# A transformer block on one core: four engines' orders laid anew, with scores between the two turned blocks of a unit

## The reference, cut to what matters

```python
def attn_ref(x, Wqkv, Wo):             # x: 32 x 256 x 128, 8 heads of 64
    qkv = einsum('bte,fe->btf', x, Wqkv)
    q, k, v = split(qkv.reshape(B, T, H, 3 * D), 3)   # then heads first
    q, k = q + pe, k + pe
    scores = einsum('bhtd,bhsd->bhts', q, k) / sqrt(D)
    probs = softmax(where(causal, scores, -inf))
    return einsum('btf,ef->bte', einsum('bhts,bhsd->bhtd', probs, v), Wo)

def ffn_ref(x, w, a1, a2, bias):
    return tanh(x @ w @ a1 @ a2 + bias)

x = x + layernorm(attn_ref(layernorm(x), Wqkv, Wo))
x = x + layernorm(ffn_ref(layernorm(x), w, a1, a2, bias))
```

## Time and profile before

| | us |
|---|---|
| median of 3 runs | 556.6 (556.47 to 557.93) |
| the profiled execution | 557.18 |
| its span, first to last instruction | 555.3 |
| TensorE busy | 523.5 (94%) |
| VectorE busy | 468.8 (84%) |
| ScalarE busy | 410.9 (74%) |
| GpSimd busy | 398.9 (72%) |

### The profile page before, as it was taken

One profiled execution on the slowest core, in us unless ns is written; L12 is line 12 of the kernel. 1 busy time (PEld: TensorE's weight loads), 2 busy tenths in 40 slices (PEclk: granted clock), 3 DMA queues, 4 the chain that ended last, 5 costly groups with the idle time before them and its releaser, 6 DMA issues.

```text
span 555.3 us, 18471 instructions
## 1 busy us (share of the span) xinstructions
PE 523.5 (94%) x5363; PEld 427.2 (77%) x5363; DVE 468.8 (84%) x2063; ACT 410.9 (74%) x1507; POOL 398.9 (72%) x650
## 2 busy tenths in 40 slices
PE   8799999999999999999999999999999999999771
PEld 4588888788888878888887887888788888878650
DVE  4988898888889888888988888898888889888723
ACT  2777878778787877878787787877778787777730
POOL 3535777777777777777778777777877777785644
PEclk9999999999999999999999999999999999999966
DMA  5100011100001010000101010010000001100000
GB/s 161 30 2 21 11 31 30 30 19 28 20 18 28 28 28 19 28 26 12 28 28 28 19 28 21 17 28 28 28 19 28 26 12 28 28 19 12 21 11 19
DMA packets 27964, 14.57 MB, mean 26 GB/s; under 512 B 1699, under 2 KB 27430, under 8 KB 27942
## 3 DMA queue, kind: packets, MB, share of 16 engines
q1 hardware_dynamic: 27510, 13.51, 8.5%
q10 hardware_dynamic: 432, 0.79, 0.4%
HBM read 10.09 MB, written 4.19 MB: 26 GB/s over the span
## 4 chain that ended last, share of the span: by engine, by line
PE 82%; ACT 9%; issue 4%; DVE 3%; DMA 1%; POOL 1%; ACTq 0%; POOLq 0%; DVEq 0%
PE turned_and_heads L935 17%; PE scores L881 15%; PE misc_bank L996 11%; PE turned_and_heads L921 9%; PE qk_bank L896 6%; ACT probs L265 5%; PE qk_bank L898 4%; PE qk_bank L897 4%; PE misc_bank L867 4%; PE misc_bank L979 3%; PE misc_bank L869 3%; PE misc_bank L868 3%; ACT vals L275 2%; ACT pt L285 1%; PE misc_bank L977 1%
## 5 line engine op out<-in xcount | busy, mean ns | idle before, releaser
L265 ACT ACTIVATE probs<-scores,neg_max 128x256 f32<-128x256 f32 (+1 forms) x512 | 209.3, 428 | 32.0 <-DVE neg_max L633 31.9
L633 DVE CUSTOM_DVE_ANT_0 scores<-scores,mask 128x256 f32<-128x256 f32 (+1 forms) x512 | 166.2, 386 | 3.2 <-PE scores L881 0.9
L643 DVE TENSOR_TENSOR qk<-qk_bank,pe 128x512 f32<-128x512 f32 x128 | 87.4, 683 | 32.9 <-PE qk_bank L898 25.3
L881 PE MATMUL scores<-qk 64*128 64x256 f32 (+1 forms) x1024 | 107.2, 337 | 5.5 <-ACT probs L265 2.5
L423 POOL TENSOR_TENSOR probs<-probs,inv_sum 128x512 f32<-128x512 f32 x126 | 101.6, 827 | 12.8 <-DVE inv_sum L649 12.8
L265 ACT ACTIVATION_READ_ACCUMULATOR probs<-scores,neg_max 128x1 f32 x512 | 108.8, 213 | 0.0
L881 PEld LDWEIGHTS scores<-qk 64*128 64x128 f32 x1024 | 88.5, 188 | 16.0 <-issue 9.8
L935 PE MATMUL turned_and_heads<-pt,vals 128*64 128x256 f32 (+1 forms) x1024 | 99.3, 337 | 1.5 <-ACT pt L285 1.5
L935 PEld LDWEIGHTS turned_and_heads<-pt,vals 128*64 128x64 f32 x1024 | 64.8, 138 | 28.3 <-issue 2.8
L283 ACT COPY pt<-turned_and_heads 128x512 f32<-128x512 f32 x128 | 76.7, 599 | 11.1 <-PE turned_and_heads L921 11.0
L896 PE MATMUL qk_bank<-xt_hi,w_hi 128*128 128x256 f32 x256 | 81.2, 317 | 2.0 <-DVE qk L643 1.2
(11 more groups left out here) (87 smaller groups left out, 863.2 us busy)
## 6 DMA issues: line engine op xcount, KB each, us to landing
x_in<-in_x SPq DMA_DIRECT2D x32, 128.0 KB, 2.2
x_res<-in_x SPq DMA_DIRECT2D x32, 128.0 KB, 2.1
out_x<-x SPq DMA_DIRECT2D x32, 128.0 KB, 1.8
w_raw<-in_w_qkv_t ACTq DMA_DIRECT2D x3, 256.0 KB, 3.7
pe<-pe_table SPq DMA_DIRECT2D x1, 256.0 KB, 5.6
wo<-in_w_o_t SPq DMA_DIRECT2D x1, 256.0 KB, 4.0
mask<-causal_mask SPq DMA_DIRECT2D x1, 128.0 KB, 5.5
w_sb<-in_w SPq DMA_DIRECT2D x2, 64.0 KB, 3.8
```

The lines of the kernel that those rows point to most:

```text
L265: ins = nc.scalar.activation(probs[k][j][:, h, lo:hi], s_bank[j][:, h, lo:hi], ACT.Exp, bias=neg_max[k][j][:, i:i + 1], scale=-1.0, accum_ ...
L633: ins = nc.vector.tensor_tensor_reduce(some, some, mask[:, t * P:2 * P], -1.0, HIGHEST, ALU.add, ALU.min, neg_max[k][j][:, i:i + 1])
L643: nc.vector.tensor_tensor(qk[j][:, :], qk_bank[:, :], pe[:, :], ALU.add).then_inc(qk_kept, 1)
L881: ins = mm(s_bank[j][:, h, at:at + k_hi], qk[j][r, q_lo:q_lo + P], qk[j][r, T:T + k_hi], start=(at == 0), stop=True, skip_group_check=True)
```

## The change

In the period, TensorE's order becomes, for k = 0: qk(1,0), heads of unit 0 of the batch before, values, qk(1,1), turned block, scores, turned block, transposes of x and y, heads of unit 1, feed-forward, qk of the next batch; and for k = 1: projection, qk, turned block, scores of the next batch, turned block, values. Scores now stand between the two turned blocks of a unit. ScalarE takes over the scaling of pair 0 (`scale_probs`, four instructions a unit), VectorE all copies of heads. The orders of ScalarE, VectorE and GpSimd are rearranged to suit; VectorE's `drain()` goes. The start loads the weights' first two parts through SyncE and four other things through ScalarE's queue behind one small exponential, and takes the low part of the first x before the second weight remainder. The end is written anew, with more warm-up matmuls, the last projection into `qk_bank` in place of `misc_bank`, and without its wait for batch 30's tanh.

```diff
@@ scalar @@
+            act.wait_ge(zeros_set, 2)
+            nc.scalar.activation(touched[:, :], eps[:, :], ACT.Exp)
+            act.dma_start(ident[:, :], ident_dram).then_inc(ident_in, 16)
...
+            def scale_probs(b, k):
+                act.wait_ge(inv_found, pairs(b, k, 1))
+                for t, (lo, hi) in enumerate(((0, T), (T, SC))):
+                    for h in range(2):
+                        some, i = probs[k][0][:, h, lo:hi], 2 * t + h
+                        ins = nc.scalar.mul(some, some, inv_sum[k][0][:, i:i + 1])
+                ins.then_inc(scaled[0], 1)
...
             def slot(b, k):
                 if k == 0:
+                    scale_probs(b.plus(-1), 0)
+                    exps(b.plus(-1), 1, 1)
+                    keep_attn(b.plus(-2))
+                    keep_turned(b.plus(-1), 0, 0)
+                    scale_probs(b.plus(-1), 1)
                     keep_turned(b.plus(-1), 0, 1)
...
@@ vector @@
-            def scale_probs(b, k):
-                dve.wait_ge(inv_found, pairs(b, k, 1))
...
-            def keep_heads(b):
+            def keep_heads(b, k):
...
             def slot(b, k):
                 if k == 0:
+                    stats_x(b.plus(2))
+                    stats_attn(b.plus(-2))
...
@@ tensor @@
             def slot(b, k):
                 if k == 0:
                     make_qk(b, 1, 0)
+                    make_heads(b.plus(-1), 0)
                     make_vals(b, 1)
+                    make_qk(b, 1, 1)
                     turn_probs(b.plus(-1), 1, 0)
-                    make_qk(b, 1, 1)
-                else:
+                    make_scores(b, 1)
+                    turn_probs(b.plus(-1), 1, 1)
                     turn_x(b.plus(1))
                     turn_y(b.plus(-2))
...
@@ tensor, end @@
                 make_attn(last.plus(-1), 1)
+                warm_up(4, qk_bank, 256)
                 make_heads(last, 0)
+                warm_up(4, qk_bank, 256)
                 turn_probs(last, 1, 0)
```

More of the change, by code:

```diff
@@ L217, in _ @@
             load(first, x_in, x_loaded)
-            sp.dma_start(ident[:, :], ident_dram).then_inc(ident_in, 16)
+            for i in range(2):
+                part = slice(i * F, (i + 1) * F)
+                sp.dma_start(w_raw[:, part], w_qkv_t[:, part]).then_inc(w_in[i], 16)
             sp.dma_start(pe[:, :], pe_dram).then_inc(pe_in, 16)
-            sp.dma_start(mask[:, :], mask_dram).then_inc(mask_in, 16)
             load(first.plus(1), x_in, x_loaded)
@@ L286, in keep_turned @@
                                turned_banks[:, :, T:T + P].rearrange("p f (n c) -> p n f c", c=D)).then_inc(pt1_kept, 1)
-            def keep_heads(b):
-                if not b.exists():
-                    return
-                act.wait_ge(heads_made, units(b, 2))
-                wait(act, attn_made, b.times(1, -1))
-                nc.scalar.copy(heads_t[b.parity][:, 2:4, :], heads_bank[:, :].rearrange("p (j t) -> p j t", j=2)
-                               ).then_inc(heads_kept[1], 1)
             def keep_x_hi(b):
@@ L378, in end @@
                 keep_y(last.plus(-1))
-                keep_heads(last)
                 tanh(last.plus(-1))
@@ L486, in slot @@
                 if k == 0:
-                    rstd_attn(b.plus(-2))
                     make_x1(b.plus(-2))
@@ L490, in slot @@
                     norm_y(b.plus(-2))
-                    norm_ffn(b.plus(-3))
+                    make_out(b.plus(-3))
                 else:
+                    norm_x(b.plus(2))
                     scale_probs(b, 0)
-                    make_out(b.plus(-3))
-                    norm_x(b.plus(2))
+                    norm_ffn(b.plus(-2))
+                    rstd_attn(b.plus(-1))
             def split_bias():
@@ L524, in end @@
             def end():
-                rstd_attn(last.plus(-2))
+                make_out(last.plus(-3))
                 make_x1(last.plus(-2))
@@ L529, in end @@
                 norm_y(last.plus(-2))
-                norm_ffn(last.plus(-3))
-                make_out(last.plus(-3))
                 scale_probs(last, 0)
@@ L534, in end @@
                 make_x1(last.plus(-1))
+                norm_ffn(last.plus(-2))
                 norm_y(last.plus(-1))
-                norm_ffn(last.plus(-2))
                 make_out(last.plus(-2))
@@ L725, in scale_last @@
             def scale_last():
+                dve.wait_ge(scaled[1], units(last, 1))
                 dve.wait_ge(inv_found, pairs(last, 1, 2))
@@ L742, in stats_attn_last @@
                 dve.wait_ge(attn_made, B)
-                take_stats("attn", last, misc_bank[:, 0:T].rearrange("p (t e) -> p t e", t=TT))
+                take_stats("attn", last, qk_bank[:, 0:T].rearrange("p (t e) -> p t e", t=TT))
             def norm_attn_last():
@@ L788, in begin @@
                 take_w_rest(0)
+                keep_x_lo(first)
                 take_w_rest(1)
-                keep_x_lo(first)
-                stats_x(first.plus(1))
                 take_w_rest(2)
@@ L794, in begin @@
                 keep_qk(first, 0, 0)
+                stats_x(first.plus(1))
                 wait_stats("x", first.plus(1))
@@ L838, in end @@
                 moments_last("y", last)
+                stats_ffn(last.plus(-1))
                 moments_last("ffn", last.plus(-1))
@@ L892, in make_qk @@
                 for part in range(2):
+                    if b.is_first() and k == 0 and j == 0:
+                        pe_eng.wait_ge(w_hi_made, part + 1)
+                        pe_eng.wait_ge(w_lo_made, part + 1)
                     p = 2 * k + j
@@ L981, in make_ffn, with make_attn_last @@
                 ins.then_inc(ffn_made, 1)
+            def make_attn_last():
+                pe_eng.wait_ge(heads_kept[0], B)
+                pe_eng.wait_ge(heads_kept[1], B)
+                pe_eng.wait_ge(qk_kept, 4 * B)
+                for t in range(TT):
+                    for p in range(PAIRS):
+                        ins = mm(qk_bank[:, t * E:(t + 1) * E], heads_t[1][:, p, t * P:(t + 1) * P], wo[:, p, :],
+                                 start=(p == 0), stop=(p == PAIRS - 1))
+                ins.then_inc(attn_made, 1)
             def make_attn(b, t):
```

187 lines of the change are left out of this document (89 added, 98 removed).

## The result

| | before | changed |
|---|---|---|
| median of 6 runs each | 557.43 (556.47 to 560.17) | 553.19 (552.12 to 553.95) |
| the profiled execution | 557.18 | 553.95 |
| its span | 555.3 | 552.1 |
| start: to the first projection | 36.51 | 42.07 |
| period, mean of 29 | 16.20 | 16.06 |

The ratio is 0.9918, with a 95% interval of 0.9892 to 0.9943. The kernel is faster by 0.8%. I had forecast 2.2%: the direction is right and the size is not (553.19 still lies inside the stated range of 535 to 554, at its upper edge). The three lower rows say where the difference lies (negative is faster): start +5.6 where the sum had 0, periods 29 x -0.14 = -4.1 where it had -6.7, end -4.6 where it had -5.2. Together -3.1; the spans differ by -3.2, the same to rounding.

The account below looks back on a forecast made before the run. TensorE's ring of some 18 blocks was taken as the bound. Span 555.3, periods -6.7, start 0, end -5.2 gave 543.4; plus 1.9 outside the span, less 0.6 to the median, 544.7; forecast 544.5 us, range 535 to 554.

Parts of the forecast that it names:

- Net 0, bounds -1.5 and +1.5: Start: first qk block some 0.8 us earlier from loading, first turned block about 0.9 later, cancelling out.
- (a): Values of t=0 on TensorE no longer wait for ScalarE's attn copy: -0.19 us a batch.
- (b): Scores of unit 1 no longer wait for unit 0's second exponentials: -0.36 us a batch.
- (c): TensorE neighbours: fewer array-shape changes at seams between scores, turned, projection and qk blocks; together -0.31 us a batch, bounds 0 and -0.45.
- (d): New TensorE stall before heads of unit 1, behind turned block and ScalarE's pt copies (chain 1.59): +0.51 us, bounds 0.4 and 0.7.
- (e): Unit 1's first turned block waits for VectorE's heads_t copy: +0.14 us a batch, bounds 0 and 0.4.
- (f): ScalarE scaling pair 0: 0.36 and 0.26 per instruction, 2.5 us a batch, hidden by scores and values, costing nothing.
- My three terms, -2.2, -3.5 and -0.4: End: shorter stretch before last heads -2.2; full-clock blocks to last projection -3.5; closing chain's two short TensorE blocks 0.4.
- Small waits everywhere with a clock that falls in the end: Rival: small waits at five places, clock falling in the end; period 16.1, end -2, about 551.5 us; chance 0.20.
- The slower rival: GpSimd's root steps delay VectorE's chain up to the heads_t copy; at 0.6 late period 16.6, 563 us; chance 0.10.
- Rival 3: Neighbouring TensorE blocks' shapes don't count, seam savings fall away; period 16.34, 555.5 us, no change; chance 0.07.
- rivals 1 and 2: No new stall: period 15.6, about 534.5 us, chance 0.14; small waits everywhere: about 551.5, chance 0.20.

Follow-up runs that it names:

- e5_half_pt: Changed kernel with ScalarE's first copy of turned weights for unit 1's second pair halved (stale numbers there); span 542.1 us, period 15.86.
- e4_heads_copy: Changed kernel with VectorE's copy of unit 0's heads moved before the y statistics and one reciprocal moved; 548.10 us, ratio to before 0.9813.
- e8_half_scale: Changed kernel with ScalarE scaling only the 128-column parts of pair 0, the other parts' factor left out; 552.30 us, period 16.07.
- e6_cold_end: Changed kernel without the end's six groups of warm-up matmuls; 553.28 us, end 45.4 against 44.3.
- e9_warm_end: Changed kernel plus first-slot warm-ups, first-slot VectorE reorder, earlier heads copy and more end warm-ups; 542.94 us, against 544.18 without the extra end warm-ups.
- e2_dve_start: Changed kernel with VectorE's first slot alone reordered: first row_max earlier, second qk copy between the two row_max; 549.30 us.

## Why the prediction was wrong in size

**The step that failed is the start.** The prediction put it as "Net 0, bounds -1.5 and +1.5". It measured +5.6 in the one profile and, from first scores on, +5.5 and +3.7 in the two. I had named the cause of the second gap (x_lo behind two row_max) and that scores of unit 1 stand ahead, and priced them at 0.9. The first and longer gap, of 2.54, I had not seen: on VectorE the qk copy stands behind the statistics and the maxima of both pairs. The order's part was 1.6, and the earlier loads gave nothing back: the first qk block started 0.5 earlier, but its second half waited for the weight remainder and the first scores began 0.1 later than before. What I had not priced at all is what an idle TensorE in a start costs beyond the gap itself: the clock, another 2.1 to 3.9. I had looked at the clock only for the end, where it had fallen before. With the start at the mean of these two measurements, +4.6, the forecast would have been 549.1; with the misses of the period (2.6) and of the end (0.6) it would have been 552.3, 0.9 from the median.

**The period, -0.14 where I had -0.23.** Point by point, by the table above:

- (a) held: values follow their turned block 0.52 later and no longer 0.72, -0.20 (forecast -0.19).
- (b) and scores in (c) held: -0.56 (forecast -0.54). Scores take 1.38 start to start.
- The rest of (c) was too good. The turned blocks' opening gap is not half a seam each: they gained 0.05 in all beyond (a), not 0.10. The projection gained 0.17, not 0.09, but the qk block behind it gives 0.07 back (0.88 where its like takes 0.81), and the two values blocks cost 0.03 more. Each seam is real; how it divides between the two blocks was guessed.
- (d) held: turned block to heads 1.60 (forecast 1.59), and e5_half_pt shows that it is this chain.
- (e) had the right place and was too small: 0.19 where I had 0.14. e4_heads_copy shows it.
- (f) held: 0 for the period, by e8_half_scale. Its size was low: four records run 1.48, and the next instruction starts 1.38 behind the first (218.34 to 219.72), where I had 1.24. The Trainium skill (ScalarE: Activation LUTs, section What ACT_TABLE_LOAD costs), which the prediction names beside its 0.36 without using it, would have given it: 280 ns + 0.833 ns a column with one pointer operand, less 93 ns of overlap, makes an estimate of 0.40 and 0.29, in all 1.39 for two of each; the trace agrees.

The row of ScalarE's timeline in the changed kernel, and what follows it:

```profile
218.34 1.48 ACT L281 ACTIVATE probs<-probs,inv_sum 128x256 f32<-128x256 f32 x4
219.72 0.46 ACT L269 ACTIVATE probs<-scores,neg_max 128x256 f32<-128x256 f32 x1
```

**The end, -4.6 where I had -5.2, right for partly wrong reasons.** My three terms, -2.2, -3.5 and -0.4, add up to -6.1; the -5.2 was taken below them without a term that says why. From the thirtieth projection to the heads of the last batch's unit 0 it took 19.67 us (507.80 to 527.47) where it had been 21.35 (506.36 to 527.71): -1.7, near the -2.2. From there to the last projection 9.58 (to 537.05) where it had been 11.72 (to 539.43): -2.1, where I had -3.5 for a held clock. The closing chain gave 0.8, where I had 0.4. The warm-ups are only 1.1 of it (e6_cold_end); most of the 2.1 comes without them: even in e6_cold_end these two points are 9.90 apart. There the y transposes of the batch before no longer stand between the last turned block and the heads, nor its feed-forward product between the heads and the projection, and both turned blocks run at the full clock (0.59 each, 0.90 before): the granted clock is 0.83 between these two points (525.62 to 535.52) where the kernel before had 0.56 (527.71 to 539.43). What gives it that clock without warm-ups was not tried apart. The rest of the held clock came with e9_warm_end and, without more warm-ups, in the one profile of e5_half_pt.

**The rivals.** Small waits everywhere with a clock that falls in the end (551.5) came nearest in time, but not in kind: the period was 16.06, near its 16.1, while the end gained and the start lost. The slower rival did not happen: GpSimd's first root step takes 0.20 in attn as well (against 638 ns in the earlier trace rows). VectorE no longer scales beside it, as the rival's counter-argument had it; that this is the reason was not tried apart. Timeline of GpSimd in the changed kernel:

```profile
223.40 0.20 POOL L411 TENSOR_TENSOR attn_var_eps<-attn_moments,eps 128x2 f32<-128x2 f32 x1 [1.14 <-DVE attn_moments L591]
```

Rival 3 is out: scores blocks with a turned block behind them are 0.07 shorter each. In the chances, forecast and rivals 1 and 2 add up to 0.83 and not 0.81; nothing hangs on it.

## What to carry to other kernels

When an order made for the steady loop is also used for its first slots, price the start by itself: lay each engine's first slot against TensorE's, look for idle time that the loop's cover would hide, and price it at the gap plus the matmuls behind it at 1.2 GHz. Where a gap can't be removed, matmuls on zeros into a free bank can fill it: in the start they kept the clock in all five profiles that had them. Half a fill is not to be relied on: with a gap of 1.2 us left open in the end the clock fell in nine profiles of ten, and in the one with all gaps filled it stayed. And a busy share of 86% says nothing on whether an engine is a bound: halving one job of it, and separately halving the one copy at which TensorE waits, told the two apart in a run each.

## What was not expected of the hardware

- The granted clock in the start is not the same from one execution to the next: with identical code the stretch from 16 to 32 us had 0.79 and 0.57 in one profile and 0.79 and 0.79 in another, and the span was 2.5 us shorter in the second. A single profile does not price such a start.
- The clock fell in this start behind one gap of 2.54 us between dense blocks, and in e2_dve_start behind gaps of 1.22, 1.52 and 0.88; the kernel before kept it there with gaps of up to 1.22. In the end it fell behind gaps of 0.44 and 1.20 us around short turned blocks; the same turned blocks with warm-ups in all the gaps kept it, and so did one profile (e5_half_pt) with the gaps open.
- A change of array shape between neighbouring blocks costs about 0.07 for scores and 0.17 for the projection; of the latter 0.07 moves to the qk block behind it when the change is gone.
